# Mamba block and mixture of experts on one core: the inputs times D are added to state 0's product by VectorE, not turned by TensorE

## What is computed

```
def step(h, t):
    dt_t, B_t, C_t, x_t = t
    dA = jnp.exp(dt_t[..., None] * A)
    h = h * dA + dt_t[..., None] * B_t[:, None, :] * x_t[..., None]
    y = jnp.einsum('bds,bs->bd', h, C_t)
    return (h, y)
...
y = jnp.swapaxes(ys, 0, 1) + xc * D_skip
y = y * jax.nn.silu(z)
```

## Time and profile before

| What | Value |
|---|---|
| Median of 3 runs | 1285.68 us (1285.03 to 1286.23) |
| The profiled execution: its own time | 1286.74 us |
| The profiled execution: span from the first to the last instruction | 1284.8 us |
| Mean granted clock of TensorE | 0.979 of full speed |
| Matmuls, transposes among them | 7422 |
| Transposes of the skip (L1350) | 128, 8 a step |

### The profile page before, as it was taken

How to read it: one execution, slowest core, us unless ns; L and a number is a source line. 1 busy time by engine, 2 the same in 40 slices (tenths; PEclk the granted TensorE clock), 3 DMA queues, 4 the chain that set the end, 5 groups by cost and what they waited for, 6 DMA issues and landing times.

```text
span 1284.8 us, 24309 instructions
## 1 busy us (share of the span) xinstructions
PE 1197.1 (93%) x7422; PEld 1029.2 (80%) x7422; DVE 995.6 (77%) x1800; ACT 1089.1 (85%) x2656; POOL 1019.4 (79%) x760
## 2 busy tenths in 40 slices
PE   5677989999999999999999999999999999998988
PEld 3466778888888888888888888888888888787876
DVE  2587987889797887879788887978889796887733
ACT  4888999899898989989898998989899998988621
POOL 2489798888888988888898888889888887888621
PEclk8797999999999999999999999999999999999999
DMA  2511102112221312222121222213121221203010
GB/s 69 199 58 52 65 19 105 46 52 90 67 92 34 100 43 64 79 68 91 42 94 43 69 72 69 92 36 98 43 75 67 68 83 53 87 36 99 17 50 17
DMA packets 33927, 86.83 MB, mean 68 GB/s; under 512 B 3592, under 2 KB 16512, under 8 KB 31360
## 3 DMA queue, kind: packets, MB, share of 16 engines
q1 hardware_dynamic: 33792, 85.20, 20.2%
HBM read 67.76 MB, written 4.84 MB: 57 GB/s over the span
## 4 chain that ended last, share of the span: by engine, by line
PE 67%; DVE 8%; issue 4%; ACT 2%; POOL 2%; DMA 2%; DVEq 0%; SPq 0%; ACTq 0%; POOLq 0%
PE psy L1359 11%; PE psx L1340 10%; PE pst L1220 8%; PE psb L1220 7%; PE psb L1214 6%; PE psf L1214 5%; PE pst L1214 4%; DVE h L1095 4%; PE psf L1308 2%; PE psf L1314 2%; PE psf L1258 2%; PE psf L1247 2%; PE psb L1314 2%; DVE acc L1059 2%; PE psb L1207 1%
## 5 line engine op out<-in xcount | busy, mean ns | idle before, releaser
L631 POOL TENSOR_TENSOR hC<-h,bC 128x1024 f32<-128x1024 f32 x256 | 604.5, 2368 | 126.1 <-DVE h L1095 116.8
L1095 DVE TENSOR_TENSOR_SCAN h<-dA,state,psx 128x256 f32<-128x256 f32 x896 | 597.2, 726 | 102.3 <-PE psx L1340 94.4
L871 ACT ACTIVATE dA<-dt,neg_a 128x256 f32<-128x256 f32 x896 | 380.1, 500 | 0.0
L1340 PE MATMUL psx<-ident,bxT 128*128 128x128 f32 x1792 | 270.5, 278 | 34.1 <-DVE h L1095 28.7
L1340 PEld LDWEIGHTS psx<-ident,bxT 128*128 128x128 f32 x1792 | 215.7, 143 | 74.4 <-issue 29.6
L1359 PE MATMUL psy<-ident,hC 128*128 128x128 f32 x2048 | 267.7, 274 | 3.9 <-POOL hC L631 3.9
L1359 PEld LDWEIGHTS psy<-ident,hC 128*128 128x128 f32 x2048 | 235.7, 142 | 10.6 <-POOL hC L631 4.7
L859 ACT ACTIVATE bxT<-uTs,BT 128x512 f32<-128x512 f32 x352 | 232.4, 715 | 5.9 <-PE psx L1340 3.1
L1220 PE MATMUL pst<-w_b_sb,cbc 128*128 128x256 f32 x480 | 110.8, 379 | 0.0
L1220 PEld LDWEIGHTS pst<-w_b_sb,cbc 128*128 128x128 f32 x480 | 90.1, 190 | 11.7
L882 ACT ACTIVATE psx<-dt,neg_a 128x256 f32<-128x256 f32 x128 | 55.3, 463 | 49.7 <-DVE h L1095 49.7
(11 more groups left out here) (178 smaller groups left out, 1894.5 us busy)
## 6 DMA issues: line engine op xcount, KB each, us to landing
bC<-bc_scratch SPq DMA_DIRECT2D x64, 512.0 KB, 4.0
cbc<-cw_scratch SPq DMA_DIRECT2D x15, 1024.0 KB, 4.7
uk<-sp_l SPq DMA_DIRECT2D x16, 512.0 KB, 6.3
xf<-in_x SPq DMA_DIRECT2D x16, 256.0 KB, 2.7
xk<-xn SPq DMA_DIRECT2D x16, 256.0 KB, 4.3
un<-bc_scratch SPq DMA_DIRECT2D x16, 256.0 KB, 4.1
xb<-in_x SPq DMA_DIRECT2D x16, 256.0 KB, 5.3
out<-x SPq DMA_DIRECT2D x16, 256.0 KB, 2.2
```

Source lines behind the costliest of these rows:

```text
L631: nc.gpsimd.tensor_tensor(hC[:, s % RC], h[:, ring(s)], bC[:, g % RINGG, s % G:s % G + 1, :].to_broadcast([P, NJ, T]), ALU.mult).then_inc( ...
L871: last = nc.scalar.activation(dA[:, s % RA, j, :], dt[:, n[1], j, :], ACT.Exp, scale=neg_a[:, j, s:s + 1])
L1095: last = nc.vector.tensor_tensor_scan(h[:, r, j, :], decays, inputs, state[:, b, j, s:s + 1], ALU.mult, ALU.add)
L1340: last = nc.tensor.transpose(psx[bx_bank(fill)][:, k, j * P:(j + 1) * P], bxT[:, s % RX, j, c:c + P], ident[:, :])
```

## The change

VectorE adds `sk` to hC of state 0, in place, at the start of part 1 of turn 1, ahead of the scan of state 1, part 1. For that it waits for GpSimd's product of state 0 (`hc_done`) and for `skip_ready`, and it now signals `skip_added`. TensorE's `add_skip` is gone; `sum_states` of state 0 is the first to write psy and takes over the wait for `yg_done`, beside one for `skip_added`. GpSimd's `weigh_u` of state 4, in turn 1, waits for `skip_added`.

```diff
                         if made_at(k) == s:
+                            if s == 1:
+                                pool.wait_ge(skip_added, count(1, n, 1))
                             weigh_u(k, n)
...
             def main(s, n, part):
                 b, r = n[1], ring(s)
+                if part == 1 and s == 1:
+                    dve.wait_ge(hc_done, count(S, n, 1))
+                    dve.wait_ge(skip_ready, count(1, n, 1))
+                    nc.vector.tensor_tensor(hC[:, 0], hC[:, 0], sk[:, :, :], ALU.add).then_inc(skip_added, 1)
                 fill = HALVES * s + part
...
-            def add_skip(n):
-
-                pe.wait_ge(skip_ready, count(1, n, 1))
-                pe.wait_ge(yg_done, count(2, n, 0))
-                for j in range(SUB):
-                    for i in range(NJ):
-                        last = mm(psy[j][:, i * P:(i + 1) * P], sk[:, i, j * P:(j + 1) * P], ident[:, :],
-                                  is_transpose=True, start=i == 0, stop=False, skip_group_check=True)
-                last.then_inc(skip_added, 1)
-
             def sum_states(s, n):
                 pe.wait_ge(hc_done, count(S, n, s + 1))
+                if s == 0:
+                    pe.wait_ge(skip_added, count(1, n, 1))
+                    pe.wait_ge(yg_done, count(2, n, 0))
                 for j in range(SUB):
                     for i in range(NJ):
                         last = mm(psy[j][:, i * P:(i + 1) * P], hC[:, s % RC, i, j * P:(j + 1) * P], ident[:, :],
-                                  is_transpose=True, start=False, stop=s == S - 1, skip_group_check=True)
+                                  is_transpose=True, start=s == 0 and i == 0, stop=s == S - 1, skip_group_check=True)
...
                 if part == 1:
-                    if s == 2:
-                        add_skip(n)
                     if s >= 2:
                         sum_states(s - 2, n)
```

## The result

| What | Before | After |
|---|---|---|
| Median, runs on one chip | 1285.95 us (1285.03 to 1288.75, 4 runs) | 1313.4 us (1311.96 to 1320.04, 4 runs) |
| Ratio of after to before | | 1.0226, 95% interval 1.0198 to 1.0255 |
| Profiled execution: own time, span | 1286.74 us, 1284.8 us | 1313.69 us, 1312.0 us |

So the direction was right and the size was not: 27.5 us instead of 13.8, and 1313.4 lies above the range. The span grew by 1312.0 - 1284.8 = 27.2 us.

What follows compares the result with a forecast made beforehand. It took a step as `turn_y`'s offset, set by VectorE or ScalarE, `pr` and ScalarE's copy, plus 58.9 us. Delays of 7.7 + 4.0 + 0.6 + 1.5 = +13.8 on 1285.68 gave about 1299.5 us, range 1289 to 1309.

Steps and rivals of the forecast that it cites:

- Add, eight regular steps: VectorE's add delays `pr` and `turn_y`: +1.54 us in steps like 9, +1.35 in steps like 12; 7.7 and 4.0 us.
- All other steps and the closing: Step 15 taken like step 9, 1.5 us; steps 0, 1, 2 and 14 taken at nothing, within 0.5 each way.
- Rival 1: TensorE alone sets the pace, so all 14.0 us of removed transposes are won: 1271.7 us; chance 0.06.
- The chain in a step: From GpSimd's product of state 0 through add, scans, gate products, logits and `lgm` to `pr`: 5.79 us.
- rival 3: VectorE's add takes 1.90 us, held up by GpSimd or otherwise: 8.0 us more, 1307.5 us; chance 0.14.
- Rival 2: The shift is taken up later, in TensorE's 0.77 us idle at step starts: 9.2 back, 1290.3 us; chance 0.10.
- Rival 4: Nothing moves: VectorE catches up before `lgm`, or the product of state 0 comes earlier: 1285.7 us; chance 0.08.
- is late of itself: ScalarE in step 10 is already late, so the add costs only +0.20 us; with steps 6 and 8, 0.6.
- the stretch still 58.9: TensorE from `turn_y` to the next step's first fill is full and keeps its 58.9 us.
- Removed: 8 transposes a step ... Gain by the rows: nothing: TensorE's skip transposes, 0.875 us a step, win nothing: TensorE comes to `turn_y` earlier and waits there for ScalarE.
- I let the new idle time cost no clock: TensorE's new idle time costs no clock, as it was 1.00 with TensorE busy for only 15.31 of 16.60 us.

Runs made afterwards that it cites:

- transposes alone: Changed kernel without the add and its waits, 64 waits added at TensorE's start, so inputs times D left out: 1279.79 us against 1287.63 before.
- add alone: Changed kernel with TensorE's 8 transposes a step kept by turning state 0 twice; only the add and GpSimd's wait are new: 1304.32 us, ratio 1.0155.
- the 64 instructions: Changed kernel with 64 instructions of long-fulfilled waits at TensorE's start, moving its loop back to its old place in the code: 1309.64 us, ratio 1.0179.
- the copy earlier: Kernel before with ScalarE's copy of the gate's input ahead of the decays of state 5: 1284.99 us, ratio 0.9988.
- the add in its later place: Changed kernel with the add behind `lgm` in turn 2, no GpSimd wait, 64 instructions at TensorE's start: 1287.83 us against 1284.12 before.
- the moved before: Kernel before with 192 idle instructions ahead of TensorE's loop, putting its start where the changed kernel has it: 1301.87 us against 1287.63.

## Why the prediction was right in kind and wrong in size

| Term, steps 3 to 13 unless named | Forecast | Measured |
|---|---|---|
| Removed transposes, their time | 0 | -0.8 (transposes alone) |
| Add, eight regular steps (3, 4, 5, 7, 9, 11 to 13) | 11.7 | 10.5 (`turn_y`, add alone) |
| Add, steps 6, 8, 10 | 0.6 | 2.3 (`turn_y`, add alone) |
| Stretch behind `turn_y` | 0 | 1.7 (add alone) |
| Removed transposes, their place in the code | not there | 9.1 (after against the 64 instructions) |
| Clock behind the new idle time | 0 | 3.0 (steps 5 and 11) |
| All other steps and the closing | 1.5 | 0.6 |
| Sum | 13.8 | about 27 |

The first row stands outside the sum, since the add alone hides the transposes as well.

**Right.** What bounds the kernel: `turn_y` waits for ScalarE's copy, and that for `lgm`, so 14 us of TensorE's busy time were worth next to nothing in the steady steps. Rival 1 needed `turn_y` not to be held by the copy; in the eleven steps 3 to 13 the transposes alone show 0.8 us where it gives 11 x 0.875 = 9.6. Going by TensorE's busy share, the highest of all, the time would have come out at 1271.7; the measurement decides against that. The chain in a step held to 0.14 us: from the product's end to `pr` 5.72 us, forecast 5.79; the shift of `turn_y` in step 9 1.40, forecast 1.54. The add took 1.22 as the earlier trace rows had it, and rival 3 fell because GpSimd waits; without that wait it comes true, and worse. Rival 2 fell: the idle time of 0.77 at each step's start is still there. Rival 4 fell with `turn_y`'s shift.

**Off in size.** Steps 6, 8 and 10 were to lose 0.2 each, since ScalarE "is late of itself" there; they lost 0.65 to 1.05. That reading had the wrong cause: with the copy earlier, where TensorE itself sets `turn_y`, these steps still reach it at 16.55, 16.01 and 16.67 and all others at 15.05 to 15.09, so it is TensorE that is late there, behind its jump. And "the stretch still 58.9" holds to 0.1 in the other steps; in steps 5, 7, 9 and 11 it became 59.2 where the clock stayed at 1.00, also with the add in its later place, and not with the transposes alone. What in that stretch makes the 0.35 was not settled. Together 3.4 us too little, against 1.2 too much in the regular steps.

**Wrong.** The step that failed is "Removed: 8 transposes a step ... Gain by the rows: nothing". It costed the instructions by their time alone. Their removal also moved everything behind them in TensorE's code, the loop's start with it, to a place from which the next 16 KB arrive too late after each jump (in step 6 the transfer is at 503.88, TensorE's last instructions before the stop at 502.90): 9.1 us, a third of the loss, with nothing about it in the rows of before that I read. The second is "I let the new idle time cost no clock". The row that I took it from had TensorE busy for 15.31 of 16.60 us, with no idle time in it longer than 1.21; the new one is 1.55 in one piece, behind another of 0.76, and the clock fell behind it in two of four such steps: 3.0 us. The range was built from bounds of the add, and held neither of the two.

## What to carry to other kernels

A busy share says nothing of what a removed instruction is worth (TensorE's was 93%, and transposes that took 14.0 us were worth 0.8 in steps 3 to 13): look for the wait behind it, and cost an addition by the whole chain that is queued behind it, not by its own time. When instructions are added or removed ahead of a loop, look at the first microseconds behind each jump back for idle time inside a run of like instructions (here 2.30 to 3.37 us, about 7 us into the step): if it is there, some padding ahead of the loop is worth a trial. Idle time that a change puts on an otherwise full TensorE can have a price in clock beside its own length (here a clock of 0.51 came with 1.55 us of it in steps 5 and 11, and 1.00 stayed in steps 7 and 9), and the windows show whether it does.

## What the runs showed that was not expected

- TensorE stood still for 1.2 to 3.7 us behind a loop's jump for want of code, or not at all, by 64 instructions far ahead of it; in before, 192 idle instructions alone made steps 3 to 13 12.7 us longer.
- Each jump back cost TensorE another 0.8 to 1.3 us of idle time in before as well, under the name of a scan or of ScalarE.
- The granted clock fell to 0.50 during or right behind two of the three stops in after and in the moved before, so that step 6 of after had another 6.8 us at the lower level.
- The same idle time of 1.55 was followed by a fall in steps 5 and 11 of after, in both executions that were profiled, and in no step with the transposes kept. What tells steps 5 and 11 from 7 and 9 stays open.
- A wait that was added, GpSimd's, saved far more than it cost: without it the add took 2.90 instead of 1.22 us, and steps 3 to 13 859.58 us instead of 839.61 (the two runs with the 64 instructions).
